# First chunk of a fused scan and mixture-of-experts kernel: sine table as products of powers, weight low parts spread later

## The reference

```
x  = x + layernorm(mixer(layernorm(x)))      # linear recurrence of 64 modes + D*u
x  = x + layernorm(moe(layernorm(x)))        # 8 experts, all of them for every token
mixer: Bu = u B^T ; h = causal convolution of Bu with Re(eig^t) ; y = h C^T + D*u
       eig = (1 - i w)/(1 + i w), w = imag(fft(a_full)), |eig| = 1
moe:   g = x Wgate[e], u = x Wup[e], h = silu(g)*u, out = sum_e cw[e] * (h Wdown[e])
       cw = softmax(x Wr) * softmax(x Wg / 0.1), normalised over the 8 experts
```

## Time and profile before

| | us |
|---|---|
| median of 3 runs (1112.18 to 1113.23) | 1112.43 |
| profiled execution | 1113.27 |
| its span, first to last instruction | 1111.4 |
| around the span (1113.27 - 1111.4) | 1.87 |
| PE busy / DVE busy / ACT busy / POOL busy | 1094.8 / 941.4 / 744.6 / 719.2 |

### The profile page before, as it was taken

How to read it: one execution, slowest core, us unless ns; L and a number is a source line. 1 busy time by engine, 2 the same in 40 slices (tenths; PEclk the granted TensorE clock), 3 DMA queues, 4 the chain that set the end, 5 groups by cost and what they waited for, 6 DMA issues and landing times.

```text
span 1111.4 us, 16965 instructions
## 1 busy us (share of the span) xinstructions
PE 1094.8 (99%) x4833; PEld 896.1 (81%) x4833; DVE 941.4 (85%) x1815; ACT 744.6 (67%) x1435; POOL 719.2 (65%) x886
## 2 busy tenths in 40 slices
PE   8899999999999999999999999999999999999997
PEld 5777888888888888888888888888888888888886
DVE  7999898897988979788897988979788897987866
ACT  5786676757667586676757667586676757666553
POOL 2785766748567575766748567575766748556454
PEclk9999999999999999999999999999999999999999
DMA  4430413313142221413213142221313213131110
GB/s 138 132 87 9 117 48 96 76 35 100 39 105 66 73 74 36 115 48 96 76 32 103 39 105 67 71 76 43 107 48 96 76 32 102 39 95 48 47 50 20
DMA packets 182285, 79.66 MB, mean 72 GB/s; under 512 B 124560, under 2 KB 160048, under 8 KB 182192
## 3 DMA queue, kind: packets, MB, share of 16 engines
q1 hardware_dynamic: 182192, 78.57, 26.5%
HBM read 59.14 MB, written 19.40 MB: 71 GB/s over the span
## 4 chain that ended last, share of the span: by engine, by line
PE 88%; issue 0%; POOL 0%; DVE 0%; POOLq 0%; ACT 0%; DVEq 0%; ACTq 0%
PE u L396 10%; PE g L397 10%; PE g L396 10%; PE u L397 10%; PE y L397 10%; PE y L396 10%; PE g L398 10%; PE u L398 10%; PE y L398 10%; PE n_ps L485 0%; PE n_ps L486 0%; PE m_ps L464 0%; PE m_ps L463 0%; PE m_ps L457 0%; PE m_ps L458 0%
## 5 line engine op out<-in xcount | busy, mean ns | idle before, releaser
L1500 POOL TENSOR_TENSOR hid_lo<-hid,hid_hi 128x512 fp32r<-128x512 f32 x256 | 341.0, 1332 | 306.6 <-ACT hid_hi L781 306.1
L775 ACT ACTIVATE gate<-g 128x512 f32<-128x512 f32 x512 | 306.0, 598 | 313.6 <-PE g L398 312.8
L1115 DVE TENSOR_TENSOR hid<-gate,u 128x512 f32<-128x512 f32 x512 | 348.0, 680 | 145.7 <-ACT gate L775 110.0
L781 ACT ACTIVATE hid_hi<-hid 128x512 fp32r<-128x512 f32 x512 | 319.6, 624 | 20.0 <-DVE hid L1115 19.3
L1124 DVE TENSOR_TENSOR hid_lo<-hid,hid_hi 128x512 fp32r<-128x512 f32 x256 | 218.4, 853 | 0.2
L396 PE MATMUL u<-xe_hi,w_hi 128*128 128x512 f32 (+1 forms) x516 | 201.0, 389 | 2.9 <-DVE hid L1115 2.7
L396 PE MATMUL g<-xe_hi,w_hi 128*128 128x512 f32 (+1 forms) x516 | 200.4, 388 | 0.3 <-DVE xe_lo L1251 0.3
L397 PE MATMUL g<-xe_lo,w_hi 128*128 128x512 f32 (+1 forms) x516 | 200.1, 388 | 0.0
L397 PE MATMUL u<-xe_lo,w_hi 128*128 128x512 f32 (+1 forms) x516 | 200.0, 388 | 0.0
L398 PE MATMUL u<-xe_hi,w_lo 128*128 128x512 f32 (+1 forms) x516 | 199.9, 387 | 0.0
L398 PE MATMUL g<-xe_hi,w_lo 128*128 128x512 f32 (+1 forms) x516 | 199.9, 387 | 0.0
(11 more groups left out here) (251 smaller groups left out, 1200.8 us busy)
## 6 DMA issues: line engine op xcount, KB each, us to landing
cw_b<-cw_scratch SPq DMA_DIRECT2D x128, 256.0 KB, 3.4
x_sb<-x_in SPq DMA_DIRECT2D x16, 256.0 KB, 3.2
out_scratch<-acc_t SPq DMA_DIRECT2D x60, 64.0 KB, 1.9
ffn<-out_scratch SPq DMA_DIRECT2D x15, 256.0 KB, 2.7
x_out<-o_sb SPq DMA_DIRECT2D x15, 256.0 KB, 2.2
xn_scratch<-mix_t SPq DMA_DIRECT2D x56, 64.0 KB, 2.2
feat<-xn_scratch SPq DMA_DIRECT2D x14, 256.0 KB, 2.6
y_scratch<-mix_t SPq DMA_DIRECT2D x56, 64.0 KB, 1.9
```

Of the source, the lines that this page charges most:

```text
L775: nc.scalar.activation(gate[:, k % 2, :], g_ps[k % 2][:], ACT.Silu).then_inc(gate_ready, 1)
L781: nc.scalar.activation(hid_hi[:, slot(c, k), :], hid[:, slot(c, k), :], ACT.Copy).then_inc(hi_ready, 1)
L1115: nc.vector.tensor_tensor(hid[:, slot(c, k), :], gate[:, k % 2, :], u_ps[k % 2][:], ALU.mult).then_inc(hid_ready, 1)
L1500: nc.gpsimd.tensor_tensor(hid_lo[:, slot(c, k), :], hid[:, slot(c, k), :], hid_hi[:, slot(c, k), :].bitcast(f32), ALU.subtract).then_inc(l ...
```

## The change

All of it lies in the head, in chunk 0's items and in chunk 1's mixer, which is worked inside them.

1. The table. VectorE doubles the fine powers to 16 steps, not 32 (one `tensor_scalar` for both halves instead of two; the norm is corrected once), squares all 17 fine powers four times to get the coarse ones (steps of 16), and forms 256 columns of `trig` as two outer products of 16 x 16 and a sum. The second 256 columns come from turned coarse powers in the same way, between `leave` of the first half and `enter` of the second.
2. The head. `WARM` 7 to 5. ScalarE rounds piece 0 before the layernorm of chunk 0, which it does in two pairs of tiles; TensorE makes low part 0 before the turn. Bu is made in two halves right behind the copies. Low parts 1 to 6 move behind it, 7 and 8 behind items 0 and 1, as do the rounding of pieces 7 and 8 and their copies on ScalarE.
3. Waits by piece, for the loads of a slot and for the low parts.
4. `LATE_SPLITS` from (3 to 11, 13, 14, 15, 19, 21, 22) to (5, 6, 7, 9, 11, 13, 14, 15, 17, 19, 21, 23, 25, 26, 27).
5. Steps move: the softmax products and weights, the first weighing, `stats_x` and `norm_x` of chunk 2, and chunk 1's mixer from `merge` to `turn_y`, all later, mostly by one item; from `own_residual` on chunk 1's steps move earlier. z of chunk 1, done by ScalarE with a sum on VectorE, becomes four VectorE instructions from PSUM; its shift is added on GpSimd at the end.
6. SP loads expert 5 behind the spread of e = 3, expert 6 behind chunk 2's block store and its load.

```diff
-WARM = 7
-LATE_SPLITS = (3, 4, 5, 6, 7, 8, 9, 10, 11, 13, 14, 15, 19, 21, 22)
+WARM = 5
+LATE_SPLITS = (5, 6, 7, 9, 11, 13, 14, 15, 17, 19, 21, 23, 25, 26, 27)
-FIRST_X_AT = {... "merge": 7, "enter_cos": 8, "enter_sin": 8, "scan": 9, "leave": 10, ... "c": 14, "y": 15}
+FIRST_X_AT = {... "merge": 8, "enter_cos": 9, "enter_sin": 9, "scan": 10, "leave": 11, ... "c": 15, "y": 16}
-FIRST_OWN_AT = {"softmax": 1, "peak": 2, "silus": 3, "exps": 4, "products": 5, "weights": 6, "weigh": 10}
+FIRST_OWN_AT = {"softmax": 1, "peak": 2, "silus": 3, "exps": 4, "products": 6, "weights": 7, "weigh": 11}
...
@@ tensor @@
             keep_warm(WARM)
-            early_turn_x()
             pe.wait_ge(minus_ready, 1)
             make_lo(0)
-            early_bu()
+            early_turn_x((0, 1))
+            early_turn_x((2, 3)).then_inc(xn_turned, 1)
+            pe.wait_ge(small_loaded, 32)
+            pe.wait_ge(trig_link, 1)
+            early_bu(FIRST_HALF)
+            early_bu(SECOND_HALF).then_inc(bu_ready, 1)
             make_lo(1)
-            make_lo(2)
...
                     if first and k < NB:
                         item_gate_up(k)
+                        if k < PE_PIECES - HEAD_PIECES:
+                            make_lo(HEAD_PIECES + k)
...
@@ scalar, items @@
                     silu(c, k, first)
+                    if first and k < PE_PIECES - HEAD_PIECES:
+                        round_piece(2, k + 1)
+                        keep_lo(HEAD_PIECES + k)
...
@@ vector, table @@
+            last = low[:, 1:3, :]
+            for level in range(3):
+                nxt = coarse[level % 2]
+                nc.vector.tensor_tensor(squares, last, last, ALU.mult)
...
+            def products(t):
+                nc.vector.tensor_tensor(square(part_a), coarse_by(t, 0), fine_by(1), ALU.mult)
+                return nc.vector.tensor_tensor(square(part_b), coarse_by(t, 1), fine_by(2), ALU.mult)
...
+            then(products(ahead))
+            nc.vector.tensor_tensor(trig[:, FIRST_HALF], part_a, part_b, ALU.add).then_inc(trig_half, 1)
```

More of the change, by code:

```diff
@@ L413, in make_lo, with early_turn_x, early_bu @@
                 nc.tensor.matmul(dst[:], minus[:], w_hi[:, e, cols], start=False, stop=True).then_inc(lo_made, 1)
[L415 to L423, removed]
+            def early_turn_x(tiles):
+                pe.wait_ge((x_pair, xn_ready)[tiles[0] // 2], 1)
+                for j in tiles:
+                    last = nc.tensor.transpose(n_ps[:, j * P:(j + 1) * P], xn[:, j, :], ident[:])
+                return last
+            def early_bu(cols):
+                pe.wait_ge(x_copied, 1 if cols == FIRST_HALF else 2)
+                return nc.tensor.matmul(m_ps[:, cols], proj[:, 0:P], hid[:, 0, cols], start=True, stop=True)
             def early_skip(tiles):
@@ L507, in gate_up @@
                         pe.wait_ge(used, UNITS * c + k - 1)
+                    if first and b == 0:
+                        wait_piece(e, off // F)
                     cols = slice(off + b * P, off + (b + 1) * P)
@@ L518, in down @@
                     pe.wait_ge(lo_dve, N_DVE_LO * c + lo_count(k))
+                if first and b == 0:
+                    wait_piece(e, 2)
                 if b == 0 and not (first and e < 2):
@@ L1190, in _ @@
                 old, new = slice(1, n + 1), slice(n + 1, 2 * n + 1)
-                nc.vector.tensor_scalar(v_cos[:, old], low[:, 1, old], si, None, ALU.mult)
-                then(nc.vector.tensor_scalar(v_sin[:, old], low[:, 0, old], si, None, ALU.mult),
+                then(nc.vector.tensor_scalar(turn[:, :, 0:n], low[:, 0:2, old], si, None, ALU.mult),
                      *steps_x.get((n, 0), ()))
-                nc.vector.scalar_tensor_tensor(out=low[:, 0, new], in0=low[:, 0, old], scalar=co, in1=v_cos[:, old],
-                                               op0=ALU.mult, op1=ALU.subtract)
@@ L1196, in _ @@
-                then(nc.vector.scalar_tensor_tensor(out=low[:, 1, new], in0=low[:, 1, old], scalar=co,
-                                                    in1=v_sin[:, old], op0=ALU.mult, op1=ALU.add),
+                if n == 2:
+                    square_norm()
+                nc.vector.scalar_tensor_tensor(out=low[:, 1:3, new], in0=low[:, 1:3, old], scalar=co,
+                                               in1=turn[:, :, 0:n], op0=ALU.mult, op1=ALU.add)
+                then(nc.vector.scalar_tensor_tensor(out=low[:, 0, new], in0=low[:, 0, old], scalar=co,
+                                                    in1=turn[:, 1, 0:n], op0=ALU.mult, op1=ALU.subtract),
@@ new lines, in _ @@
+            last = low[:, 1:3, :]
+            for level in range(3):
+                nxt = coarse[level % 2]
+                nc.vector.tensor_tensor(squares, last, last, ALU.mult)
+                if level == 0:
+                    early_shift_x()
+                links[0] += 1
+                nc.vector.scalar_tensor_tensor(out=nxt[:, 1], in0=last[:, 1], scalar=2.0, in1=last[:, 0],
+                                               op0=ALU.mult, op1=ALU.mult).then_inc(trig_link, 1)
+                dve.wait_ge(trig_link, links[0])
+                then(nc.vector.tensor_tensor(nxt[:, 0], squares[:, 0], squares[:, 1], ALU.subtract))
+                last = nxt
@@ new lines, in _ @@
+            ahead, there = coarse[1], slice(STEP, STEP + 1)
+            c_far, s_far = high[:, 0:1], high[:, 1:2]
+            nc.vector.tensor_tensor(squares, last, last, ALU.mult)
+            nc.vector.scalar_tensor_tensor(out=ahead[0:NS, 1], in0=last[0:NS, 1], scalar=-2.0, in1=last[0:NS, 0],
+                                           op0=ALU.mult, op1=ALU.mult)
+            then(nc.vector.scalar_tensor_tensor(out=ahead[NS:P, 0], in0=last[NS:P, 1], scalar=2.0, in1=last[NS:P, 0],
+                                                op0=ALU.mult, op1=ALU.mult))
@@ new lines, in _, with square, coarse_by, fine_by @@
+            nc.vector.tensor_tensor(ahead[0:NS, 0], squares[0:NS, 0], squares[0:NS, 1], ALU.subtract)
+            then(nc.vector.tensor_tensor(ahead[NS:P, 1], squares[NS:P, 0], squares[NS:P, 1], ALU.subtract))
+            def square(t):
+                return t.rearrange("p (a b) -> p a b", b=STEP)
+            def coarse_by(t, h):
+                return t[:, h, 0:STEP].unsqueeze(2).broadcast_to([P, STEP, STEP])
+            def fine_by(h):
+                return low[:, h, 0:STEP].unsqueeze(1).broadcast_to([P, STEP, STEP])
```

245 lines of the change are left out of this document (119 added, 126 removed).

## The result

| | kernel before | changed kernel |
|---|---|---|
| median, us | 1112.68 (4 runs) | 1121.4 (4 runs, 1119.04 to 1121.5) |
| ratio, 95% interval | | 1.0067 (1.0054 to 1.0081) |
| profiled execution / span | 1113.27 / 1111.4 | 1121.4 / 1119.6 |

The changed kernel is slower by some 0.7%: 7.5 us by the ratio, 8.7 us between the two medians. Its median lies 8.6 us above my highest bound. The busy line hardly moves against the earlier trace rows: the work is the same, and the loss is idle time and lost clock.

What follows compares the result with a forecast made beforehand. TensorE's work plus its idle time before about 120 us was taken as the bound. Head 1.8, items 0 to 3 -4.1 and gaps 5.2 made 2.9 us less, 1109.5 us by median, range 1106.8 to 1112.8.

Steps and rivals of the forecast that it cites:

- my highest bound: Whole kernel: upper end of the predicted range for the time, 1112.8 us.
- What bounds the kernel, and where the time is set: Whole kernel: TensorE's work plus idle time; all idle time that can move lies before about 120 us.
- The head: Before the first item: faster table and earlier Bu start `enter` and the first item 1.8 us sooner (bounds 1.6 and 2.5).
- Items 0 to 3: Chunk 0's first items: low parts 7 and 8 and waits for ScalarE cost 4.1 us (bounds 2.2 and 4.9).
- The gaps, and what closes: TensorE's gaps between chunk 0's items: 5.2 of 7.2 us close (bounds 2.5 and 7).
- move to the items 17 to 27: GpSimd's later pieces: stalls move there, where TensorE sets the pace, costing only what exceeds VectorE's slack.
- the less hopeful of my two readings: GpSimd's moved pieces: by the exclusive-lock rule nothing is saved, since the same 15 pieces are made.
- My second rival: Chunk 0's items: gaps close by half only, waits pushed to items 10 to 14; 1.1 us less, 1111.3; chance 0.23.
- edits at no cost: Waits by piece, chunk 1's z, the added bias step and SP's expert 6 load: no cost expected if cover holds.
- No PE idle behind 120 us: Sign expected in the changed profile: TensorE has no idle time after 120 us.
- The late piece: Item 28's u waits for piece 22, or expert 6's load is late: 0 to 2 us, up to 1111.4; chance 0.06.
- The slower rival: Items 0 to 3 paid in full, VectorE doesn't catch up, gaps stay: 1114.7 up to 1115.5 us; chance 0.08.

Runs made afterwards that it cites:

- e6: e5 with the step order, GpSimd piece places and SP expert loads of the kernel before; 1110.29 us, ratio 0.9981.
- e3: The changed kernel with chunk 3's x loaded by SP ahead of the stores; 1116.18 us (two groups, 1116.1 and 1117.5), ratio 1.003.
- e5: e3 with low parts 7 and 8 back in the head; 1113.3 us (groups 1112.1 and 1113.3), ratio 1.0008.
- e2: The changed kernel with GpSimd's last six pieces earlier, at items 18 to 23; 1116.58 us, ratio 1.0037.
- e9: e5 with GpSimd's piece places and SP's expert loads of the kernel before, steps in the changed order; 1110.80 us.
- e10: e6 with GpSimd's piece places and SP's expert loads of the change, steps as in the kernel before; 1113.43 us.
- e11: e6 with chunk 0's softmax products one item later, from 5 to 6; 1109.85 us, ratio 0.9965.
- e12: e11 with statistics and norm of chunk 2's x two items later as well; 1109.85 us, ratio 0.9965.
- e7: e3 with GpSimd's 15 late pieces on 8 columns, not 512, the rest zeroed by a memset (computation incomplete); 1116.69 us, ratio 1.0042.
- e8: The kernel before with GpSimd's 15 late pieces on 8 columns, the rest zeroed (computation incomplete); 1115.94 us, ratio 1.0041.
- e1: The changed kernel with chunk 0's first weighing back at item 10, not 11; 1119.1 us, ratio 1.0055.

## Why the prediction was wrong, step by step

**What bounds the kernel, and where the time is set: right.** The steady stretch is unchanged, and all 8 us came ahead of 130 us, though the last 3.4 came a little beyond the 120 that I named, with TensorE's wait that ends at 124.10.

**The head: right.** `enter` at 12.60 (forecast 13.1, bounds 12.4 to 13.2), the first half of the table ready at 12.1 (12.1), the first item at 24.51 (24.7). Bu starts at 11.38 (11.3), and the next matmul follows 0.94 later (12.32), near the 0.85 of the full clock, not the 1.7 that I took. The window that answers the earlier trace rows has the clock at 1.00:

```profile
12.00:13.00 1.00, 1.00 (x6) 0.65 (x4) 0.69 (x5) 0.84 (x3) 0.00 (x0) 1.00 0.74 225
```

e6 fits the term: 1110.29 against 1112.1, 1.8 us, with the early load and the z steps in it.

**Items 0 to 3: right in size.** Forecast 4.1 us; e3 against e5 gives 4.26 at item 5 and 2.4 to 4.0 in the time. Each wait for ScalarE was 0.49 instead of 0.7. At item 5 the lag was 2.2, of a forecast 2.3.

**"The gaps, and what closes": the step that failed.** I put +5.2 us there. Measured from item 5 on, the changed kernel lost 6.0 (lag 2.2 to 8.2). Up to item 17 the closing went better than the end shows: with the full clock (e2) items 5 to 17 take 30.06 us against 31.48, 1.4 us gained of the 5.2, and the rest of the way lost it again. Four things stand in its place.

- *The lock, which I set aside.* I wrote that the stalls of the pieces "move to the items 17 to 27", and priced them at what exceeds VectorE's slack, as if there were slack. I never counted it. The row to count was there, in the windows of the kernel before (below): VectorE has 1.08 us free in 90 to 105, where GpSimd makes no piece, and the changed kernel puts three there. e5, e6, e9 and e10: 2.8 us for the places. The Trainium skill (SBUF — State Buffer, two separate sides) has the rule, an exclusive lock held for the whole instruction. The traces agree: `den`, 4 columns, 1.26 us, until GpSimd's pieces end, and at 94.50 GpSimd held in its turn, 2.19 for 1.29. Even the less hopeful of my two readings, that nothing is saved, was too kind: the pieces saved 1.0 to 1.3 us up to item 17 and cost 2.7 to 4.2 behind it.
```profile
90.00:105.00 15.00, 14.21 (x64) 11.30 (x65) 13.92 (x26) 9.92 (x21) 6.84 (x5) 1.00 0.00 1
```

- *A gap that closes isn't kept.* The 1.28 us wait of bu went as forecast. I counted it as gain in full, while VectorE was the engine that set the pace (14.81 of 15.00 in the earlier trace rows). There an item's time is VectorE's work, and moving steps about mostly moves the wait. e11 and e12 kept 0.4 to 0.6 of 1.26 by item 31. My second rival had this (waits pushed to items 10 to 14, where they now stand), with too small a price.
- *The load behind a store.* I followed expert 6 through SP's list, as one row had a wait for weights, and put SP's changes under "edits at no cost". I did not follow the loads of x in chunk 1. e3 takes 4.1 us away, the largest single term, by moving the load ahead of the store. But this isn't an effect of the new order as far as the rows show: e2, with the load in its old place, has a fast store and loses nothing. What the changed kernel's profile has beside it is a store that takes 3.46 us and not 1.98. e12, which has the places of the kernel before and e6's order but for two steps, has an even longer one (3.73) and no loss from it, as its load goes first. Whether the change makes the slow store more frequent stays open: three of its four executions lie at 1121.4 to 1121.5 and one at 1119.04, and only one was profiled. "No PE idle behind 120 us" was the sign that failed here.
- *The clock.* A wait of 2.5 us is followed by the half clock in some executions (the changed kernel, e3), and not in others (e2, e5, e9); 1.4 to 1.6 us (e3 against e2). I had priced the clock only in the head.

The late piece was among the rivals and the signs of being wrong, priced at 0 to 2 us of wait; it waited 1.73. Its mechanism and place were right. I gave it 0.06, and took it for the only effect of the late places, while e2 shows that without it the stretch is as long.

**The slower rival** was the right sign with too small a price: 1114.7 to 1115.5, from items 0 to 3 paid in full and gaps that stay. e3, with the load ahead of the store, is near that time at 1116.2, but by luck: its condition, `act_lo` still too late at item 5, wasn't met, as the wait of bu went, and the loss came from the pieces and the clock.

**The parts in one sum**, by the ratios (0.1% is 1.1 us), each undone on top of the last: x loaded behind the store, slow store and clock with it, 1.0067 - 1.0030, 4.1 us; low parts 7 and 8 behind items 0 and 1, 1.0030 - 1.0008, 2.4; places of the pieces and order of the steps, 1.0008 - 0.9981, 3.0; new head 0.9981 - 1, -2.1, with what the z steps and the early load (0.7 in the profiles) give against the kernel before. Together 7.5, against a forecast of -2.9. The 1.4 to 1.6 of the low clock are in these terms, and the ratios of e3 and e5 come from different chips. Each term is good to about 1 us, as the intervals are 0.1% to either side. Whether e5's upper group is again the low clock wasn't shown; its profile is of the lower one.

The head is worth having: e11 has it with the old places, the early load, the z steps and one step moved, at 1109.85. That this is close to the time that I forecast for the whole change is chance.

## What to carry to other kernels

Where an engine has next to nothing free (here VectorE, 0.19 of 15.00 us), a wait removed in its consumer is worth only what work it takes off that engine; moving steps mostly exchanges one wait for another, so don't count the whole wait as saved (here a third to a half was). When work of GpSimd is moved, add up VectorE's free time in the stretch where it arrives before calling it slack. A load that stands behind a store in a queue pays for whatever that store takes, and stores here took 1.95 to 3.73 us: put a load that nothing holds back ahead of the store. And before a loss is put down to a delay, count from the same item in both kernels: the store here stood 9.04 us behind item 31 in either.

## What was unexpected in the hardware

A memset on GpSimd held a VectorE instruction of 3 columns for its whole length, in e7; first VectorE, then GpSimd:

```profile
6.81 6.64 DVE L1207 TENSOR_SCALAR low<-low,ang 128x3 f32<-128x3 f32 x1
6.93 6.50 POOL L1562 MEMSET w_lo<- 128x7680 f32 x1
```

It ends at 13.45, the memset at 13.43; e8 has the same (6.59 beside 6.50). This cost the head of both kernels some 7 us. The Trainium skill (SBUF — State Buffer, two separate sides) counts VectorE instructions in a two-port mode among those that can take the lock or be held by it. The one held here is a `TENSOR_SCALAR`; in which mode it ran, no row shows. By the same section of the Trainium skill the one that starts first gets the lock, and here VectorE's row starts 0.12 us before the memset's (0.06 in e8) and is still the one held.

The issues of four small stores on SP took 3.46 us in the changed kernel and 3.73 in e12, and 1.95 to 1.98 in the other profiles:

```profile
105.70 3.73 SPq L289 DMA_DIRECT2D y_scratch<-mix_t  x4
```

In e1 the issues took 1.98 and the next transfer still went out 2.6 us behind them, 1.4 in the kernel before. No run tested why.
